# A three-layer graph network on one core: the end of a layer re-ordered, and one fifth of layer 1's one-hot instructions moved from VectorE to ScalarE

## The reference

```python
for k in range(3):
    e = edge_vector @ edge_W[k] + edge_b[k]
    msg = relu(x[src] + e)
    agg = segment_sum(msg, dst, num_segments=n)
    z = (1.0 + eps[k]) * x + agg
    h = relu(batch_norm(z @ W1[k] + b1[k]))
    x = relu(layer_norm(h @ W2[k] + b2[k]) * ln_g + ln_b)
out = layernorm(x_input + x)
```

## Time and profile before

| | |
|---|---|
| median of three runs | 1322.03 us (1318.77 to 1322.22) |
| the profiled execution | 1316.41 us, of which the span from first to last instruction is 1314.5 us |
| busy share of the span | TensorE 91%, VectorE 81%, GpSimd 67%, ScalarE 49% |
| mean granted TensorE clock | 0.96 |
| TensorE's gathers: layer 1, 2, 3 begin at | 384.5, 711.7, 1012.2 us |

### The profile page before, as it was taken

The page is one execution under the profiler, slowest core; times in us unless marked ns, Lnnn a source line. Parts: engine busy times, 40 slices in busy tenths (PEclk is TensorE's granted clock), DMA queues, the critical chain, the costliest instruction groups (busy, mean ns, idle before and its releaser), DMA issues.

```text
span 1314.5 us, 36888 instructions
## 1 busy us (share of the span) xinstructions
PE 1199.7 (91%) x13740; PEld 1015.6 (77%) x13740; DVE 1061.0 (81%) x2044; ACT 649.1 (49%) x1255; POOL 886.7 (67%) x842
## 2 busy tenths in 40 slices
PE   3999999999996899999995899999996899999995
PEld 1555555555566798989994899999995898999994
DVE  8889988899877989999987566777776658788887
ACT  2666666666643344444452344444542434545443
POOL 0555666678877777777744777777763777777770
PEclk8999999999998999999996899999996899999997
DMA  8787888888988878787885676777776577788771
GB/s 181 242 275 262 277 295 286 295 292 266 315 264 274 253 232 243 236 246 231 246 263 149 200 233 214 237 235 229 225 238 172 174 229 215 241 240 251 227 222 32
DMA packets 253572, 310.05 MB, mean 236 GB/s; under 512 B 53837, under 2 KB 170623, under 8 KB 253415
## 3 DMA queue, kind: packets, MB, share of 16 engines
q1 hardware_dynamic: 205646, 212.37, 52.5%
q0 software_dynamic: 33280, 82.06, 19.6%
q10 hardware_dynamic: 14489, 13.40, 4.1%
HBM read 200.17 MB, written 107.55 MB: 234 GB/s over the span
## 4 chain that ended last, share of the span: by engine, by line
PE 51%; issue 15%; DVE 14%; POOL 13%; DMA 3%; ACT 2%; ACTq 2%; DVEq 0%; SPq 0%
PE ps L1553 21%; POOL rows L649 9%; PE ps L1580 6%; PE ps L1570 5%; POOL srt_dram L665 4%; PE ps L1524 3%; PE ps L1526 3%; PE ps L1525 3%; PE ps L1527 3%; PE ps L1528 3%; DMA rows<-table_dram,src_i 2%; PE ps L1589 1%; DVE terms L1198 1%; DVE terms L939 1%; DVE terms L1097 1%
## 5 line engine op out<-in xcount | busy, mean ns | idle before, releaser
L649 POOL DMA_INDIRECT rows<-table_dram,src_i x416 | 424.8, 1021 | 182.6 <-issue 176.5
L665 POOL DMA_INDIRECT srt_dram<-region,pos_i x208 | 230.6, 1109 | 148.3 <-ACT region L735 61.7
L649 POOL DMA_INDIRECT rows<-x_dram,src_i x208 | 229.1, 1102 | 63.4 <-issue 62.2
L1553 PE MATMUL ps<-xs,early_words 125*128 125x128 bf16 x2720 | 255.8, 223 | 10.9 <-issue 10.9
L1553 PE MATMUL ps<-xs,region 125*128 125x128 bf16 x2584 | 237.7, 220 | 12.9 <-issue 12.8
L1553 PE MATMUL ps<-xr,early_words 125*128 125x128 bf16 x1360 | 245.7, 223 | 0.0
L1553 PEld LDWEIGHTS ps<-xs,early_words 125*128 125x128 fp8e4 x2720 | 221.0, 99 | 11.2 <-issue 11.1
L1553 PE MATMUL ps<-xr,region 125*128 125x128 bf16 x1292 | 228.5, 220 | 0.0
L1553 PEld LDWEIGHTS ps<-xs,region 125*128 125x128 fp8e4 x2584 | 206.2, 98 | 13.3 <-issue 13.1
L745 ACT ACTIVATE terms<-terms 128x512 f32<-128x512 f32 x156 | 97.3, 624 | 228.8 <-DVE terms L1191 228.8
L1580 PE MATMUL ps<-hot_p,terms 128*128 128x64 f32 x1248 | 169.6, 280 | 8.4 <-issue 7.9
(11 more groups left out here) (191 smaller groups left out, 2539.4 us busy)
## 6 DMA issues: line engine op xcount, KB each, us to landing
ep_dram<-terms SPq DMA_DIRECT2D x52, 768.0 KB, 4.4
terms<-srt_dram SPq DMA_DIRECT2D x156, 256.0 KB
terms<-ep_dram SPq DMA_DIRECT2D x156, 256.0 KB
early_words<-hotrow_dram SPq DMA_DIRECT2D x156, 104.0 KB
region<-kept_dram SPq DMA_DIRECT2D x13, 576.0 KB
early_words<-kept_dram SPq DMA_DIRECT2D x13, 576.0 KB
region<-kept_dram SPq DMA_DIRECT2D x13, 560.0 KB
early_words<-kept_dram SPq DMA_DIRECT2D x13, 560.0 KB
```

What stands on the lines that cost most here:

```text
L649: pool.indirect_dma_start(rows[:, q, t * FEAT:(t + 1) * FEAT], None, source, bass.IndirectOffsetOnAxis(ap=src_i[:, c:c + 1], axis=0),).the ...
L665: pool.indirect_dma_start(srt, bass.IndirectOffsetOnAxis(ap=pos_i[:, c:c + 1], axis=0), stage_s[:, q, t, :], None).then_inc(scattered[q], 16)
L1553: ins = nc.tensor.matmul(bank(q)[:, c:c + FEAT], hot_g[v % 2][0:SLICE, h, at:at + P], x_part(part, FIRST[t] + k), start=k == 0 and part == ...
```

## The change

ScalarE takes over the last (k = 4) of the five comparisons of each half, for bodies 1 to 12 of layer 1, in two steps: the absolute difference into a new fp16 tile `away`, then relu(1 - that). `hot_here` is raised by 8 from either engine. `zero` is split off from `flush`; at the end of a layer it comes later, and not at all in layer 3. The norm of the last pair (with `final_sum` in layer 3) comes after the flushes and the tail's sums. ScalarE's `hidden` of the tail comes before the last pair's `features`. In the last body TensorE's `hidden` of the pair comes before the gather of quad 3. On ScalarE the loop over layers is written out, layer 1 wholly, and `features` has no `act.If` any more.

```diff
+            def last_hots(j, h):
+                act.wait_ge(relB_loaded[j % 2][h], (j // 2 + 1) * 16)
+                if j >= 2:
+                    act.wait_ge(hot_kept[j % 2][h], j // 2 * 16)
+                    act.wait_ge(g_filled, (j - 2) * BLOCK_QUADS + 2 * (h + 1) + BLOCK_QUADS)
+                else:
+                    for q in range(BLOCK_QUADS):
+                        act.wait_ge(scattered[q], BODIES * 16 * QUAD)
+                k = SPANS - 1
+                a, b = RUNS[h][k]
+                at, n = pair_at(a, k) * P, (b - a) * P
+                nc.scalar.activation(away[:, 0:n], relB[...], ACT.Abs, scale=-1.0,
+                                     bias=tab[:, C_NODE + k:C_NODE + k + 1]).then_inc(away_made, 1)
+                act.wait_ge(away_made, 2 * j + h - 1)
+                nc.scalar.activation(hot_g[j % 2][:, h, at:at + n], away[:, 0:n], ACT.Relu, scale=-1.0,
+                                     bias=ones[:, :], saturate=False).then_inc(hot_here[j % 2][h], 8)
...
-                for n, table in enumerate(tables):
-                    with act.If(l == n):
-                        act.dma_start(table[bass.ds(t * NT, NT), :], one(x_cur, t)).then_inc(stored, 16)
+                act.dma_start(tables[l][bass.ds(t * NT, NT), :], one(x_cur, t)).then_inc(stored, 16)
...
                 relus(l, j, 1)
+                if builds and not last:
+                    last_hots(j + 1, 0)
...
                 relus(l, j, 3)
+                if builds and not last:
+                    last_hots(j + 1, 1)
...
                 if not last:
                     relus(l, j + 1, 0)
+                else:
+                    for h in range(TAIL):
+                        hidden(l, first + h, h, first + h, tail_zh)
...
-                    with act.Fori(0, 2) as j:
-                        body(l, j, False)
-                    with act.Fori(2, BODIES - 1) as j:
-                        body(l, j, True, final=final)
+                    if l == 0:
+                        for j in range(BODIES - 1):
+                            body(l, j, j >= 2, builds=True)
+                    else:
+                        with act.Fori(0, 2) as j:
+                            body(l, j, False)
+                        with act.Fori(2, BODIES - 1) as j:
+                            body(l, j, True, final=final)
...
-                with act.Fori(0, LAYERS - 1) as l:
+                for l in range(LAYERS - 1):
                     layer(l, False)
...
+            def zero(l, j, h):
+                dve.wait_ge(z_summed, l * BLOCKS + (j * 2 + h + 1))
+                nc.vector.memset(z_bank(h), 0.0).then_inc(flushed, 1)
...
-                dve.wait_ge(z_summed, l * BLOCKS + (s + 1))
-                nc.vector.memset(z_bank(h), 0.0).then_inc(flushed, 1)
...
-                    build_hots(j + 1, 1, 2)
-                if nodes:
-                    node_norm(l, *a, b[0])
-                    node_norm(l, *b, b[0])
+                    build_hots(j + 1, 1, 2, SPANS - 1)
+                if nodes and not last:
+                    end_of_pair(l, j, final, visit)
...
                     for h in range(2, TAIL):
                         node_sum(l, first + h, h, first + h, True, tail_zh)
+                    end_of_pair(l, BODIES - 1, "later" if final else None, ((BODIES - 1) % 2, 16 * ((BODIES - 1) // 2)))
+                    if not final:
+                        for h in range(2):
+                            zero(l, BODIES - 1, h)
...
-                gather(l, j, 3)
+                if not last:
+                    gather(l, j, 3)
                 if nodes:
                     hidden(l, *a, b[0])
                     hidden(l, *b, b[0])
+                if last:
+                    gather(l, j, 3)
```

More of the change, by code:

```diff
@@ L212, in build @@
         stage_s = region[:, 0:BLOCK_QUADS * QUAD * SRT_COLS].rearrange("p (q t c) -> p q t c", q=BLOCK_QUADS, t=QUAD)
+        away = sb("away", [P, HALF * P], f16)
         hot_words = 2 * PAIRS * P // 4
@@ L344, in build @@
         s_relu = sem("s_relu")
+        away_made = sem("away_made")
         p_relu = sem("p_relu")
@@ L765, in relus @@
                 relu_p(l, j, q)
+            def last_hots(j, h):
[9 more added lines that the diff above has]
+                at, n = pair_at(a, k) * P, (b - a) * P
+                nc.scalar.activation(away[:, 0:n], relB[:, j % 2, h, (a - h * HALF) * P:(b - h * HALF) * P], ACT.Abs,
+                                     scale=-1.0, bias=tab[:, C_NODE + k:C_NODE + k + 1]).then_inc(away_made, 1)
+                act.wait_ge(away_made, 2 * j + h - 1)
+                nc.scalar.activation(hot_g[j % 2][:, h, at:at + n], away[:, 0:n], ACT.Relu, scale=-1.0,
+                                     bias=ones[:, :], saturate=False).then_inc(hot_here[j % 2][h], 8)
             def scaled(l, t, h, upto):
@@ L798, in final_deviation, with body @@
                                      bias=eps_col[0:NT, :]).then_inc(fin_std, 1)
-            def body(l, j, nodes, last=False, final=False):
+            def body(l, j, nodes, last=False, final=False, builds=False):
                 a, b = (j * 2 - 4, 0), (j * 2 - 3, 1)
+                first = NODE_TILES - TAIL
                 stored = table_ready if last else table_early
@@ L837, in layer @@
                     relus(l, 0, 0)
-                    with act.Fori(0, 2) as j:
-                        body(l, j, False)
-                    with act.Fori(2, BODIES - 1) as j:
-                        body(l, j, True, final=final)
+                    if l == 0:
[6 more added lines that the diff above has]
+                            body(l, j, True, final=final)
                     body(l, BODIES - 1, True, last=True, final=final)
                     first = NODE_TILES - TAIL
-                    for h in range(TAIL):
-                        hidden(l, first + h, h, first + h, tail_zh)
                     if final:
@@ L1180, in build_hots @@
                         tab[:, C_NODE + k:C_NODE + k + 1], None, ALU.is_equal, saturate=False)
-                if stop == SPANS:
+                if j == 0 and stop == SPANS:
                     ins.then_inc(hot_here[j % 2][h], 16)
+                elif stop == SPANS - 1:
+                    ins.then_inc(hot_here[j % 2][h], 8)
             def quad(l, j, q):
@@ L1269, in final_norm, with end_of_pair @@
                                         rstd[:, TAIL + h:TAIL + h + 1], ALU.subtract, ALU.mult).then_inc(fin_ready, 1)
+            def end_of_pair(l, j, final, visit):
+                a, b = (j * 2 - 4, 0), (j * 2 - 3, 1)
+                node_norm(l, *a, b[0])
+                node_norm(l, *b, b[0])
+                if final:
+                    slot, loaded = visit
+                    final_sum(*a, loaded, slot)
+                    final_sum(*b, loaded, slot)
             def body(l, j, flushes, nodes, builds, last=False, final=None, visit=None):
@@ L1291, in body @@
                     flush(l, j - 1, 0, first=flushes == "first")
+                    zero(l, j - 1, 0)
                     flush(l, j - 1, 1)
+                    zero(l, j - 1, 1)
                 if builds and not last:
@@ L1299, in body @@
                 if builds and not last:
-                    build_hots(j + 1, 0, 2)
+                    build_hots(j + 1, 0, 2, SPANS - 1)
                 if builds and j < 2:
@@ L1312, in body @@
                 if builds and not last:
-                    build_hots(j + 1, 1, 2)
-                if nodes:
-                    node_norm(l, *a, b[0])
-                    node_norm(l, *b, b[0])
-                if nodes and final:
-                    slot, loaded = visit
-                    final_sum(*a, loaded, slot)
-                    final_sum(*b, loaded, slot)
+                    build_hots(j + 1, 1, 2, SPANS - 1)
+                if nodes and not last:
+                    end_of_pair(l, j, final, visit)
             before_branch = done[0]
```

## The result

| | before | after |
|---|---|---|
| median | 1321.04 us (1314.38 to 1325.33, 21 runs) | 1314.09 us (1309.23 to 1321.37, 21 runs) |
| profiled execution | 1316.4 us | 1314.09 us, span 1312.2 us |
| ratio of the times | | 0.9956, 95% interval 0.9943 to 0.997 |

By the ratio the change makes the kernel 5.8 us faster (4.0 to 7.5 by the interval); the two medians are 6.95 us apart. I had forecast 18.65, and a median between 1297 and 1313 us. The sign was right, and the gain is about a third of what I forecast.

The account below looks back on a forecast made before the run. Layer 1 was taken as bound by three things within about 2 us: a chain of waits, VectorE's work and TensorE's. 14.7 + 2.5 + 1.45 = 18.65 us off 1316.4 gave 1297.8 (1303.4 off the median), range 1297 to 1313.

Parts of the forecast that it names:

- the third of the three bounds on a body of layer 1: Layer 1 after the change: TensorE needs 20.7 us a body, layer 2's pace of 21.1 less its wait.
- VectorE's bound: Layer 1 after the change: VectorE's own work takes 20.7 us a body, 22.58 less 0.77 of waiting and 1.15 of comparisons.
- rival (d): Layer 1: TensorE or the relus hold nearly today's pace, gain under 4 us, about 1320 us; chance 0.06.
- (a): GpSimd's gathers become the bound in layer 1: 8 to 9 us gained there, nothing in layer 2, about 1312; chance 0.25.
- forecast 14.7 us for layer 1's bodies: Layer 1, twelve bodies: nine at 1.25 us and three at 1.15 us saved; bounds 9 and 16.5 us.
- ScalarE written out: Layer 1: the step from quad 0's relus to the scaling falls from 3.26 to about 1.7 us.
- the 1.55 of the chain: Layer 1: the scaling comes 1.55 us earlier, so the chain of waits through a body falls from 22.58 to 21.0 us.
- The one-hots on ScalarE: Layer 1: 24 pairs of ScalarE instructions at 1.8 us each, bounds 1.4 and 2.9, costing nothing in idle time.
- rival (c): Layer 1, half 1: ScalarE's pair delays the deviations, through table loads; 19 us slower, 1341 us; chance 0.04.
- Layer 2's bodies: Layer 2: dropping the `act.If`s gives back 2.5 of the 3.2 us that TensorE waits for ScalarE's scaling.
- The ends of the layers: Reordered work at the three layer ends: 0.4, 0.95 and 0.1 us gained, 1.45 in all, bounds -0.5 and 3.5.
- The swap's price of 1.2 us in layer 3: Last body of layer 3: TensorE stands 0.9 to 1.2 us for the pair's sum ahead of the hidden layer.

Follow-up runs that it names:

- early_cols: The changed kernel with each of TensorE's column loads moved one step ahead of its use; ratio to before 0.9906.
- act_only: The kernel before with ScalarE's layer loop and layer 1's body loop written out and the store's If gone, all one-hots still on VectorE; ratio to before 0.9973.
- fewer_gathers: The changed kernel with GpSimd fetching three of the four tiles of each quad in layers 2 and 3; ratio to before 0.9712.
- early_no_swap_2: The changed kernel with columns loaded one step earlier and, in the last body, TensorE's gather of quad 3 again before the pair's hidden layer; 1300.25 us, ratio 0.9848.

## Why the prediction was wrong, step by step

**The step that failed** is the third of the three bounds on a body of layer 1: "TensorE: layer 2's 21.1 less its wait of 3.2 / 9, 20.7". It takes TensorE's pace from a layer in which the stores of one-hots don't run. In layer 1 TensorE has stops of its own at the column loads, 6.4 us over nine bodies of before (0.7 a body), 8.0 in after (0.9). A body's TensorE work without any stop adds up to 20.5 us in the chain of after, which is TensorE and its stops alone from 475 to 661 us; the stops there add 0.96 us a body, and the scatters that are longer at a load (16 of L1627, 6 of L1617) about 0.5. That comes to 21.9, and 21.86 was measured. So the term for the work was near, and the stops with what follows them, 1.4 to 1.5 us, were put at nothing.

The chain that I followed through one body of before held such a stop, and I passed over it:

```profile
545.49 0.78 issue
```

I told that part as "TensorE up to the end of the gather", and took off VectorE's bound the 0.77 us of waiting behind it without asking what had made TensorE late. The waits of TensorE I had read for layer 2 alone; the table for layer 1 has two lines of "issue", each larger than the wait for ScalarE. It also answers the argument that I held against rival (d), TensorE's idle tenth: of its waits between 400 and 690 us of before 14.8 us are for VectorE in the first bodies, 9.4 are stops and 3.9 are for ScalarE. Rival (d) named the right engine ("TensorE or the relus hold layer 1 at nearly today's pace") and got 0.06; the result lies between it and (a).

**VectorE's bound was right.** It was 22.58 - 0.77 - 1.15 = 20.7 us; with TensorE out of the way 20.85 was measured, and 21.93 with the comparisons left in. The nine bodies of after are nine times 20.85, 187.7 us, and the 9.0 us for which VectorE waits for TensorE or without a releaser: 196.7 of the 196.8. So of the forecast 14.7 us for layer 1's bodies 5.9 came (the first add of body 12 fell from 668.6 to 662.7 us), and with the loads early and nothing else altered layer 1 is 13.8 us shorter again (301.5 us in early_cols against 315.3).

**ScalarE written out.** The forecast was that the scaling comes 1.55 us earlier and TensorE stops waiting for it. Both came true: the step from the relus to the scaling is 1.6 us in the mean in after (3.26 before, about 1.7 forecast; 2.2 in act_only, where VectorE's norms come later), and the wait (3.9 us, 8 times, over nine bodies) went to none. But in act_only the body gained the 0.5 us down to VectorE's bound with all comparisons, not the 1.55 of the chain: the next bounds stood much closer than 21.0.

**The one-hots on ScalarE** cost 0.81 and 0.83 us, 1.74 from the start of the pair to its end, against my 1.8. TensorE's waits show nothing hurt behind them, and no table load was added, so rival (c) had nothing to it. The Trainium skill (ScalarE: Activation LUTs, section What ACT_TABLE_LOAD costs) gives an activation with a bias read from a column about 280 ns and 0.833 ns for each column, an estimate of 813 ns for 640 columns: the trace agrees.

**Layer 2's bodies**, forecast at 2.5 us, brought nothing. TensorE's wait for the scaling did not go: it is 8.1 us in 8 times in the profile of after (714 to 1000 us), where before had 3.2 in 9. With the fewer gathers it is gone, so what makes the scaling late there is most likely a VectorE that waits for rows, and not the `act.If`. I read 97% of TensorE's time busy as TensorE's bound; fewer_gathers shows 20.5 us a body for TensorE, and with all of GpSimd's rows it was 21.0 to 22.2, by the execution.

**Rival (a)**, with 0.25, had the right engine in the wrong layer. In layer 1 the last rows were ready 11.0 us before they were added in after (10.9 before) and still 8.2 us in early_cols, and GpSimd's mean fell with the body, from 1100 to 1065 ns, and to 1015 ns in early_no_swap_2. The equality of 16 gathers and a body, which I had put forward for it, was no bound there. In layer 2, where the rival expected nothing new, GpSimd is the bound.

**The ends of the layers**, forecast at 1.45 us with bounds of -0.5 and 3.5, measured 0.7 us alone (-1.8 to 3.2 by the interval). That is consistent with the forecast and with nothing at all. The swap's price of 1.2 us in layer 3 shows as a wait of 1.05.

## What to carry to other kernels

List the waits of every engine for the very stretch that you price, also those that the profile can't put down to anybody: an engine's own stops make a bound, and a pace from a neighbouring stretch doesn't hold them. Where several bounds lie within a microsecond, taking one away shows only the distance to the next; here early columns and ScalarE's written-out loop gave 0.5 us a body each by itself, fewer comparisons nothing on top of the loop, and the three together 1.6 us. And load what an address needs one step ahead of the work that uses it, with other work in between.

## What the runs showed of the hardware

No row shows a register load; what it costs is seen from the edits. In TensorE's queue, put directly ahead of its use, a load from SBUF stops the engine for 0.2 to 1.0 us in 14 of the 45 places in nine bodies of layer 1, where a store of 560 to 576 KB from SBUF runs twice a body, and in none of them where that store is cut to 128 columns (the DMA share is 0.82 and 0.71). Where the engine stands at a wait for VectorE's memset just ahead of the load, the load adds 0.75 us to the wait, with or without the stores, and the profile can put such a wait down to "issue". Placed ahead of a gather of some 2.6 us it costs nothing to be seen.

GpSimd's gathers took 1100, 1065 and 1015 ns in the mean in bodies of 22.43, 21.86 and 20.85 us, for the same rows. Most of them take 0.94 to 0.96 us in every one of these kernels; what differs is the share of those over 1.2 us (27% before, 22% in after, 7% in early_no_swap_2, between 450 and 650 us). So the mean isn't a price that can be multiplied. What lengthens those few wasn't tested.
